# One fused attention and expert-mixture layer: the experts' maximum product widened to 64 rows, their softmax sums put on four groups of 32 columns

## The chip, the cores and the metric

The kernel runs on one core of a Trainium2 chip. The metric is device time in microseconds of one execution; for the kernel before, the median of three timed executions is 5184.0 us (5180.48 to 5186.56).

## The reference, cut to what matters

Thirty-two sequences of 512 tokens with 256 features go through a pre-norm attention layer with 16 heads of 16 and then a pre-norm layer of gated "expert" attention with 8 heads of 64:

```python
wv = topk_mask(gl_v, 2) * sigmoid(gl_v)                  # gates of the values, 5 experts a head
xv = einsum('btd,edk->btek', x, Wv)
v = einsum('bthe,btek->bhtk', wv, xv)
scores = einsum('bhid,bhjd->bhij', q * scale, k)          # 8 heads, 512 x 512
probs = softmax(scores, axis=-1)                          # maximum, exponential, sum
attn = einsum('bhij,bhjd->bihd', probs, v)
out = einsum('bthe,bthk,ekd->btd', mask_o, attn, Wo)
```

The two things that the change touches belong to this `softmax`: the row maxima, which are taken off before the exponential, and the row sums, by which the result is divided.

## The kernel before

One sequence is called a batch. A batch's work is cut into 16 slots, and the slots of neighbouring batches overlap like a pipeline: a list of slots, each of three thirds (g = 0, 1, 2), is walked through in the same order by all five engines, and each engine issues in every third what falls there. Semaphores tie the engines together; a small helper drops waits that were already satisfied. In this text, slot n of a batch is the one in which the experts' exponentials of its step n (of 16) are made; the steps are four pairs of heads times four blocks of 128 keys.

Per slot, TensorE makes in g = 0 and g = 1 one score tile of the first attention for exponentials (L209, into the double bank `expb`) and one for its maxima (L239, into `maxb`), then the products with the values (L263 for the first attention in g = 0, L274 for the experts in g = 1). In g = 2 it makes the experts' scores for the exponentials (L223, three products in split precision of 64 rows for each of two heads, which lie in rows 0 to 63 and 64 to 127), adds the negated maxima to the same accumulation (L227: a product of 2 rows, ones times the two parts of the maxima in `mrow`), and then makes the experts' scores for the maxima of a later step (L251). `expb` and `maxb` are each one buffer: ScalarE must have read `expb` (L429, L438) and VectorE `maxb` (the maxima, L560, L566) before the next product goes into it. Around these steps lie the projections, transposes and output products (L285 to L415), a few in each slot, which share two banks in turn.

Every fourth slot (n = 1, 5, 9, 13) has the sums of one pair of heads. GpSimd has added the exponentials over the keys (L741, into `acc`: 128 partitions, two heads, 512 queries). L382 sums over the partitions: for each of the 8 blocks of 128 queries it loads the block as weights and multiplies with a column of ones, so that the sums of 128 queries come out as one column, one query on each partition. VectorE takes the reciprocal of these 8 columns (L684, `rcf`) and multiplies it into the experts' weights (L689), and only then comes to the next maxima. The gate (top two of five, L636 to L671) is VectorE's work in slots n = 11 to 14; GpSimd then makes the gated values `vh` (L754, L759) that L274 reads from slot n = 1 on.

SyncE moves the maxima to HBM and back into `mrow` (L849, L854), and starts its loop after the constants are set (L803).

Of the kernel before, what the change touches and what calls it, by code (L numbers as in the profile page):

```python
# [36 lines left out]
def program(nc, t):  # L37
    F32, BF, F32R = mybir.dt.float32, mybir.dt.bfloat16, mybir.dt.float32r
# [3 lines left out]
    with ctx:  # L42
        def sb(name, shape, dt=F32):
            return ctx.enter_context(nc.sbuf_tensor("s_" + name, shape, dt))
# [32 lines left out]
        mrow = sb("mrow", [128, 2, 512], F32R)  # L77
# [11 lines left out]
        nmf = sb("nmf", [128, 4])  # L89
        prod = sb("prod", [128, 4, 2, 64])  # L90
        xf = sb("xf", [128, 2, 512])
        xg = sb("xg", [128, 4, 400])
        cg = sb("cg", [128, 10, 64])
        top = sb("top", [128, 6])
# [9 lines left out]
        ones = sb("ones", [128, 128], F32R)  # L104
        one = sb("one", [128, 1])
        mxf = sb("mxf", [128, 2, 4, 2])
# [88 lines left out]
        def tensor(e):  # L195
            w = Once(e)
            w.wait_ge(c_weights, 11 * 16)
            for s in SLOTS:
                for g in range(3):
# [12 lines left out]
                    if g == 2 and (r := part_of(s, F, 16)):  # L212
                        b, n = r
                        pair, kc = n // 4, n % 4
                        _, before = X.next(None, a_fexp, 16 * b + n + 1)
                        if before:
                            w.wait_ge(*before)
                        w.wait_ge(d_fr[pair], 32 * (b + 1))
                        t3, kk = (4 * b + pair) % 3, slice(128 * kc, 128 * kc + 128)
                        for kp, qp in ((hi, hi), (hi, lo), (lo, hi)):  # L220
                            for u in range(2):
                                ra = slice(64 * u, 64 * u + 64)
                                e.matmul(xb[:, u, :], kp[ra, t3, 1, kk], qp[ra, t3, 0, :],  # L223
                                         start=(kp is hi and qp is hi), stop=False)
                        for u in range(2):
                            ra = slice(64 * u, 64 * u + 2)
                            m = e.matmul(xb[:, u, :], ones[ra, :], mrow[ra, pair % 2, :], start=False, stop=True)  # L227
                        m.then_inc(p_fexp, 1)
# [25 lines left out]
                    if g == 0 and (r := part_of(s, 1, 16)):  # L254
# [4 lines left out]
                        if kc == 0:  # L259
                            w.wait_ge(c_vector, 4)  # L260
                            w.wait_ge(v_tr, 4 * b + j)
# [110 lines left out]
                    if r := pair_at(s, g, FS):  # L372
                        b, pair = r
                        n = 4 * b + pair
                        bk, before = R.next(("sum", b, pair), v_sum, n + 1)
                        if before:
                            w.wait_ge(*before)
                        w.wait_ge(c_pool, 3)
                        w.wait_ge(g_add, 6 * n + 6)
                        for u in range(2):  # L380
                            for i in range(4):
                                m = e.matmul(bk[:, 4 * u + i:4 * u + i + 1], acc[:, u, 128 * i:128 * i + 128], one[:, :],  # L382
                                             start=True, stop=True)
                        m.then_inc(p_acc, 1)
# [147 lines left out]
        def vector(e):  # L532
# [3 lines left out]
            e.memset(ks[96:128, :, :].bitcast(F32), 1.0).then_inc(c_vector, 1)  # L536
            e.memset(ones[:, :].bitcast(F32), 1.0).then_inc(c_vector, 1)

# [14 lines left out]
            for s in SLOTS:  # L553
                for g in range(3):
# [72 lines left out]
                    if r := at(s, g, [(27, 2), (28, 1), (29, 1), (29, 2), (30, 0)]):  # L627
                        b, k = r
                        gl = xg[:, :, 320:400].rearrange("p i (g e) -> p e i g", e=5)
                        cm = cg[:, :, :].rearrange("p c (i g) -> p c i g", i=4)  # L630
                        b0 = NG * b
                        w.wait_ge(a_xg, 4 * b + 4)
                        if k < 2:
                            for i in (2 * k, 2 * k + 1):
# [44 lines left out]
                    if r := pair_at(s, g, FS):  # L679
# [3 lines left out]
                        w.wait_ge(v_w, n)  # L683
                        e.reciprocal(rcf[:, :, :], R.at["sum", b, pair][:, 0:8].rearrange("p (u i) -> p u i", u=2)  # L684
                                     ).then_inc(v_sum, 1)
                        w.wait_ge(v_sum, n + 1)
                        if n > 1:
# [13 lines left out]
        def gpsimd(e):  # L701
# [9 lines left out]
            for s in SLOTS:  # L711
                for g in range(3):
# [29 lines left out]
                    if r := part_of(s, 30, 12):  # L742
# [4 lines left out]
                        if n == 0 or n % 2 == 1:  # L747
                            to = vv if n == 0 else prod[:, :, :, :]
                            w.wait_ge(v_gate, NG * b + NG)
# [7 lines left out]
                        else:  # L757
                            w.wait_ge(g_val, k)
                            e.tensor_tensor(vv, vv, prod[:, :, :, :], ALU.add).then_inc(g_val, 1)  # L759
                    for pair in range(4):  # L760
# [25 lines left out]
        def sync(e):  # L786
            w = Once(e)
            e.dma_start(xn[:, :, :], t["x"][0].rearrange("(c p) n -> p c n", p=128)).then_inc(d_xin, 16)
            for dst, src in [
# [12 lines left out]
                e.dma_start(dst, src).then_inc(c_weights, 16)  # L802
            w.wait_ge(c_vector, 4)  # L803
            for s in SLOTS:
                for g in range(3):
# [37 lines left out]
                    if r := pair_at(s, g, FT):  # L843
# [9 lines left out]
                        for u in range(2):  # L853
                            e.dma_start(mrow[64 * u:64 * u + 2, pair % 2, :].bitcast(F32), maxf[pair][:, u, :]  # L854
                                        ).then_inc(d_fr[pair], 16)
# [57 lines left out]
```

## Time and profile before

| what | value |
|---|---|
| median of 3 executions | 5184.0 us (5180.48 to 5186.56) |
| the profiled execution | 5176.93 us, of which the span of the trace is 5175.1 us |
| granted TensorE clock, mean over the span | 0.933 |
| PE busy | 4895.9 us, 95% |
| DVE busy | 3104.6 us, 60% |
| ACT busy | 2355.9 us, 46% |
| POOL busy | 3759.7 us, 73% |

PE is TensorE's matmuls, PEld its weight loads, DVE VectorE, ACT ScalarE, POOL GpSimd, SP SyncE. Matmuls are pipelined, so the busy time of PE counts their latencies too; the distance from one start to the next says more than the duration of one. A matmul of 32-bit floats stands in the trace as two records, one of the split-precision type as one.

### The profile page before, as it was taken

Reading aid. Unit: us, or ns where it says so; the run is one execution under the profiler, and the core shown is the slowest. Engines: PE = TensorE matmul, PEld = TensorE weight load, DVE = VectorE, ACT = ScalarE, POOL = GpSimd, SP = SyncE. Lnnn points to the kernel's source line nnn. Section 1 sums busy time; section 2 is a strip of 40 time slices with the busy share of each in tenths; the row PEclk is TensorE's granted clock in tenths of the full one; section 3 lists DMA queues with packets and bytes.
Section 4 is the critical chain, followed back from the end, with each engine's and each line's share of the span. In section 5 each row is a group of like instructions: output and inputs, shape, how many; then the busy total and the mean of one; then the engine's idle time right before and its main releaser. Section 6 shows DMA issues by size and latency. Waiting matters only on the chain.

```text
span 5175.1 us, 63686 instructions
## 1 busy us (share of the span) xinstructions
PE 4895.9 (95%) x23424; PEld 2131.0 (41%) x23424; DVE 3104.6 (60%) x4164; ACT 2355.9 (46%) x3073; POOL 3759.7 (73%) x3149
## 2 busy tenths in 40 slices
PE   5889999999999999999999999999999999999986
PEld 2234444444444444444444444444444444444343
DVE  4566666666666666666666666656666656666431
ACT  2444444444444444444444445444444444444421
POOL 0057777877777777777787777787777787777898
PEclk7799999999999999999999999999999999999987
DMA  3211111111111111111111112111111111111000
GB/s 90 66 51 41 44 51 41 51 45 54 44 42 45 46 45 55 44 41 54 37 48 52 44 41 55 36 51 49 45 44 51 37 54 45 52 44 32 10 5 9
DMA packets 158502, 231.58 MB, mean 45 GB/s; under 512 B 21680, under 2 KB 72688, under 8 KB 158192
## 3 DMA queue, kind: packets, MB, share of 16 engines
q1 hardware_dynamic: 158192, 227.51, 15.4%
q8 instruction: 186, 3.05, 0.2%
q14 instruction: 124, 1.02, 0.1%
HBM read 140.39 MB, written 87.03 MB: 44 GB/s over the span
## 4 chain that ended last, share of the span: by engine, by line
PE 80%; DVE 12%; POOL 3%; ACT 2%; issue 2%; DMA 1%; SPq 0%; POOLq 0%; ACTq 0%; DVEq 0%
PE bank L369 9%; PE ofb L274 9%; PE oab L263 9%; PE expb L223 8%; PE expb L209 6%; PE maxb L239 6%; PE bank L296 5%; PE bank L382 5%; PE maxb L251 4%; PE bank L415 4%; DVE s_mxa L560 4%; PE expb L227 4%; PE bank L349 4%; DVE s_mxf L566 4%; PE bank L329 3%; PE bank L317 2%
## 5 line engine op out<-in xcount | busy, mean ns | idle before, releaser
L560 DVE TENSOR_REDUCE s_mxa<-maxb 128x2 f32<-128x1024 f32 x1024 | 1247.8, 1219 | 348.1 <-PE maxb L239 347.1
L429 ACT ACTIVATE s_pa<-expb 128x1024 f32<-128x1024 f32 x1024 | 1052.8, 1028 | 411.7 <-PE expb L209 399.2
L438 ACT ACTIVATE s_pf<-expb 128x1024 f32<-128x1024 f32 x512 | 524.9, 1025 | 1033.1 <-PE expb L227 1026.4
L566 DVE TENSOR_REDUCE s_mxf<-maxb 128x2 f32<-128x1024 f32 x512 | 627.0, 1225 | 593.5 <-PE maxb L251 592.4
L741 POOL TENSOR_TENSOR s_acc<-s_acc,s_pf 128x512 f32<-128x512 f32 x512 | 661.5, 1313 | 117.6 <-ACT s_pf L438 117.6
L741 POOL TENSOR_TENSOR s_acc<-s_pf 128x512 f32<-128x512 f32 x256 | 320.5, 1274 | 527.7 <-ACT s_pf L438 527.7
L774 POOL TENSOR_TENSOR s_uu<-s_uu,s_pu 128x640 f32<-128x640 f32 x448 | 693.4, 1548 | 11.0
L759 POOL TENSOR_TENSOR s_vh<-s_vh,s_prod 128x512 f32<-128x512 f32 x512 | 652.8, 1275 | 15.5
L263 PE MATMUL oab<-s_pa,s_v 128*17 128x512 f32 x4096 | 614.7, 676 | 0.0
L239 PE MATMUL maxb<-s_ks,s_qs 48*128 48x512 f32 x2048 | 483.3, 457 | 138.0 <-DVE s_mxa L560 97.0
L274 PE MATMUL ofb<-s_pf,s_vh 128*64 128x512 f32 x2048 | 564.0, 629 | 32.0 <-POOL s_vh L759 22.0
L209 PE MATMUL expb<-s_qs,s_ks 50*128 50x512 f32 x2048 | 557.0, 530 | 28.4 <-ACT s_pa L429 10.1
L780 POOL TENSOR_TENSOR s_pu<-s_ots,s_w 128x640 f32<-128x640 f32 x448 | 574.6, 1283 | 2.9
L754 POOL TENSOR_TENSOR s_prod<-s_xg,s_wvx 128x512 f32<-128x512 f32 x512 | 543.3, 1061 | 13.1
L209 PEld LDWEIGHTS expb<-s_qs,s_ks 50*128 50x128 f32 x2048 | 207.1, 194 | 575.7 <-issue 399.8
L579 DVE TENSOR_TENSOR s_lo<-bank,s_hi 128x512 fp32r<-128x512 f32 x256 | 177.1, 692 | 374.6 <-ACT s_hi L446 374.6
L715 POOL TENSOR_TENSOR s_rsa<-s_vea,s_nhalf 128x4 f32<-128x4 f32 x32 | 32.6, 1018 | 393.4 <-DVE s_nma L550 380.1
L446 ACT CAST s_hi<-bank 128x512 fp32r<-128x512 f32 x256 | 150.2, 587 | 365.0 <-PE bank L369 365.0
L239 PEld LDWEIGHTS maxb<-s_ks,s_qs 48*128 48x128 f32 x2048 | 212.6, 199 | 247.4 <-DVE s_mxa L560 150.6
L382 PEld LDWEIGHTS bank<-s_one,s_acc 128*128 128x128 f32 x2048 | 247.0, 197 | 121.2 <-DVE s_lo L579 96.6
L251 PE MATMUL maxb<-s_hi 64*128 64x512 f32 x1024 | 267.7, 520 | 23.0 <-DVE s_mxa L560 22.0
L223 PE MATMUL expb<-s_hi 64*128 64x512 f32 x1024 | 276.8, 514 | 0.7 <-DMA s_mrow<-w_maxf 0.2
(106 smaller groups left out, 6655.3 us busy)
## 6 DMA issues: line engine op xcount, KB each, us to landing
w_parts<-s_pt SPq DMA_DIRECT2D x128, 512.0 KB, 2.9
s_qs<-w_parts SPq DMA_DIRECT2D x256, 128.0 KB, 3.2
s_ks<-w_parts SPq DMA_DIRECT2D x256, 128.0 KB, 3.1
s_xn<-in_x SPq DMA_DIRECT2D x32, 512.0 KB, 4.7
s_qs<-w_parts SPq DMA_DIRECT2D x256, 64.0 KB, 3.2
s_ks<-w_parts SPq DMA_DIRECT2D x256, 64.0 KB, 3.0
s_xa<-in_x SPq DMA_DIRECT2D x32, 512.0 KB, 4.6
out_y<-s_xa SPq DMA_DIRECT2D x32, 512.0 KB, 2.9
```

The costliest lines, as they stand in the source:

```text
L209: m = e.matmul(xb[:, a, :], ks[64 * a:64 * a + 50, pr, 128 * kc:128 * kc + 128], qs[64 * a:64 * a + 50, pr, :], start=True, stop=True)
L223: e.matmul(xb[:, u, :], kp[ra, t3, 1, kk], qp[ra, t3, 0, :], start=(kp is hi and qp is hi), stop=False)
L239: m = e.matmul(mb[:, a, :], qs[64 * a:64 * a + 48, pr, 128 * i:128 * i + 128], ks[64 * a:64 * a + 48, pr, :], start=True, stop=True)
L263: m = e.matmul(oa[32 * h:32 * h + 17, :], v32[:, b % 2, kc, 4 * j + h, :], pa[:, (32 * b + 2 * n + h // 2) % 3, h % 2, :], start=(kc == 0) ...
L274: m = e.matmul(of[64 * u:64 * u + 64, :], vh[:, kc, 2 * pair + u, :], pf[:, (16 * b + n) % 3, u, :], start=(kc == 0), stop=(kc == 3))
L429: e.activation(pa[:, k % 3, :, :], xb[:, :, :], ACT.Exp, scale=0.0625).then_inc(a_aexp, 1)
L560: e.tensor_reduce(mxa[:, c, k % 4, 2 * (k // 4):2 * (k // 4) + 2], mb[:, :, :], AX.X, ALU.max, negate=True).then_inc(v_amax, 1)
L566: e.tensor_reduce(mxf[:, pair % 2, i, :], mb[:, :, :], AX.X, ALU.max, negate=True).then_inc(v_fmax, 1)
L741: e.tensor_tensor(acc[:, u, :], was, pf[:, k % 3, u, :], ALU.add).then_inc(g_add, 1)
L759: e.tensor_tensor(vv, vv, prod[:, :, :, :], ALU.add).then_inc(g_val, 1)
L774: e.tensor_tensor(uu[:, cut, :], uu[:, cut, :], pv, ALU.add).then_inc(g_mix, 1)
L780: e.tensor_tensor(to.rearrange("p i (e k) -> p i e k", k=64), ots[:, n % 2, cut, 64 * u:64 * u + 64].unsqueeze(2).to_broadcast([128, 2, 5, ...
```

## The change

L227 becomes a product of 64 rows: a new tile `mx` of 128 rows holds zeros but for rows 0, 1, 64 and 65, to which SyncE now brings the maxima, and `ones` is zero but for the same four rows. L382 swaps its operands: the stationary one is a tile of ones with 32 columns, and the moving one is `acc`, of which each quarter of every block of 128 queries goes to its own group of 32 columns; the sums of a head then stand as rows, 32 copies of each, in the four quarters of the partitions. VectorE turns them with a transpose of 32 by 32 blocks into `t1` and takes the reciprocal from there. Room for `mx` is made by letting the gate's tile `cg` share memory with GpSimd's `prod`, with a wait in the gate for it; the constants need three more memsets.

```diff
-        prod = sb("prod", [128, 4, 2, 64])
+        prod = sb("prod", [128, 640])
+        cg = prod[:, :].rearrange("p (c g) -> p c g", g=64)
+        prod = prod[:, 0:512].rearrange("p (i u k) -> p i u k", i=4, u=2)
-        cg = sb("cg", [128, 10, 64])
-        one = sb("one", [128, 1])
+        one = sb("one", [128, 32])
+        mx = sb("mx", [128, 2, 512], F32R)
...
-                            ra = slice(64 * u, 64 * u + 2)
-                            m = e.matmul(xb[:, u, :], ones[ra, :], mrow[ra, pair % 2, :], start=False, stop=True)
+                            ra = slice(64 * u, 64 * u + 64)
+                            m = e.matmul(xb[:, u, :], ones[ra, :], mx[ra, pair % 2, :], start=False, stop=True)
...
-                        bk, before = R.next(("sum", b, pair), v_sum, n + 1)
+                        bk, before = R.next(("sum", b, pair), v_sum, 2 * n + 1)
...
                         for u in range(2):
-                            for i in range(4):
-                                m = e.matmul(bk[:, 4 * u + i:4 * u + i + 1], acc[:, u, 128 * i:128 * i + 128], one[:, :],
-                                             start=True, stop=True)
+                            rows = acc[:, u, :].rearrange("p (i q t) -> p q i t", i=4, q=4)
+                            for q in range(4):
+                                m = e.matmul(bk[32 * q:32 * q + 32, 128 * u:128 * u + 128].rearrange(
+                                    "p (i t) -> p i t", i=4), one[:, :], rows[:, q, :, :], start=True, stop=True)
...
-            e.memset(ones[:, :].bitcast(F32), 1.0).then_inc(c_vector, 1)
+            e.memset(ones[:, :].bitcast(F32), 0.0).then_inc(c_vector, 1)
+            e.memset(mx[:, :, :].bitcast(F32), 0.0).then_inc(c_vector, 1)
+            w.wait_ge(c_vector, 4)
+            e.memset(ones[0:2, :].bitcast(F32), 1.0).then_inc(c_vector, 1)
+            e.memset(ones[64:66, :].bitcast(F32), 1.0).then_inc(c_vector, 1)
...
+                        w.wait_ge(g_val, 36 * b)
...
-                        e.reciprocal(rcf[:, :, :], R.at["sum", b, pair][:, 0:8].rearrange("p (u i) -> p u i", u=2)
+                        e.transpose(t1[:, 0, 0:256], R.at["sum", b, pair][:, 0:256]).then_inc(v_sum, 1)
+                        w.wait_ge(v_sum, 2 * n + 1)
+                        e.reciprocal(rcf[:, :, :], t1[:, 0, 0:256].rearrange("p (u i t) -> p u i t", u=2, t=32)[:, :, :, 0]
                                      ).then_inc(v_sum, 1)
-                        w.wait_ge(v_sum, n + 1)
+                        w.wait_ge(v_sum, 2 * n + 2)
...
-                            e.dma_start(mrow[64 * u:64 * u + 2, pair % 2, :].bitcast(F32), maxf[pair][:, u, :]
+                            e.dma_start(mx[64 * u:64 * u + 2, pair % 2, :].bitcast(F32), maxf[pair][:, u, :]
                                         ).then_inc(d_fr[pair], 16)
```

The waits of TensorE and SyncE for VectorE's constants go from 4 to 7.

## Rows read from the trace of the kernel before

**Rows 1.** The page, part 4: the chain that ended last, by engine.
```profile
PE 80%; DVE 12%; POOL 3%; ACT 2%; issue 2%; DMA 1%; SPq 0%; POOLq 0%; ACTq 0%; DVEq 0%
```

**Rows 2.** Busy time by stretch: PE, PEld, DVE, ACT, POOL, then clock, DMA, GB/s.
```profile
500.00:2500.00 2000.00, 1949.74 (x9502) 851.05 (x9501) 1253.76 (x1689) 953.69 (x1245) 1523.76 (x1273) 0.96 0.16 46
...
4950.00:5000.00 50.00, 47.69 (x199) 23.76 (x198) 19.65 (x20) 16.35 (x25) 49.29 (x40) 0.91 0.03 12
```

**Rows 3.** One batch's matmuls of L227: count, durations, first and last start.
```profile
L227 PE MATMUL expb<-s_mrow,s_ones x34: 489/497/613, 2456.1 to 2609.7; 2*128 2x512 f32 x34
```

**Rows 4.** Timeline of PE, third g = 2 of slot 5: start, length, instruction.
```profile
2508.49 0.51 PE L223 MATMUL expb<-s_hi 64*128 64x512 f32 x2
2508.83 0.40 PE L223 MATMUL expb<-s_lo,s_hi 64*128 64x512 f32 x2
2509.06 0.39 PE L223 MATMUL expb<-s_hi,s_lo 64*128 64x512 f32 x2
2509.38 0.50 PE L227 MATMUL expb<-s_mrow,s_ones 2*128 2x512 f32 x2
2509.81 0.50 PE L251 MATMUL maxb<-s_hi 64*128 64x512 f32 x2
2510.25 0.66 PE L392 MATMUL bank<-s_ident,s_osb 128*128 128x128 f32 x4
```

**Rows 5.** Timeline of PE, thirds g = 0 and 1 of slot 5.
```profile
2501.71 0.40 PE L239 MATMUL maxb<-s_ks,s_qs 48*128 48x512 f32 x2
2502.04 1.05 PE L263 MATMUL oab<-s_pa,s_v 128*17 128x512 f32 x8
2503.02 0.70 PE L369 MATMUL bank<-s_xf,s_fk 128*128 128x512 f32 x1
...
2506.62 1.95 PE L382 MATMUL bank<-s_one,s_acc 128*128 128x1 f32 x16
```

**Rows 6.** Groups by line, whole span: busy us, mean ns, idle before and releaser.
```profile
L263 PEld LDWEIGHTS oab<-s_pa,s_v 128*17 128x17 f32 x4096 | 69.8, 98 | 180.0 <-issue 180.0
...
L597 DVE STREAM_TRANSPOSE s_t<-oab 128x512 f32<-128x512 f32 x128 | 90.2, 704 | 3.5 <-PE oab L263 3.5
```

**Rows 7.** Timeline of DVE and of PE, slot 13 (sums and gate).
```profile
2583.93 0.22 DVE L649 TENSOR_TENSOR s_rk<-s_rk,s_cg 128x64 f32<-128x64 f32 x1
...
2584.30 0.22 DVE L689 TENSOR_TENSOR s_w<-s_mask,s_rcf 128x40 f32<-128x40 f32 x1
2585.50 1.23 DVE L566 TENSOR_REDUCE s_mxf<-maxb 128x2 f32<-128x1024 f32 x1 [0.98 <-PE maxb L251]
...
2583.64 0.50 PE L223 MATMUL expb<-s_hi 64*128 64x512 f32 x2
```

**Rows 8.** Busy time and clock by stretch, after sums; and one sum block.
```profile
2354.53:2361.36 6.83, 6.83 (x27) 1.86 (x24) 3.75 (x4) 4.25 (x7) 6.06 (x5) 0.50 0.03 5
...
2467.17:2474.00 6.83, 6.83 (x24) 3.23 (x23) 2.45 (x2) 2.64 (x3) 6.83 (x7) 0.50 0.00 0
...
2503.00:2517.00 14.00, 13.76 (x82) 6.51 (x78) 8.03 (x10) 7.57 (x11) 11.58 (x10) 1.00 0.19 33
...
2464.16 1.95 PE L382 MATMUL bank<-s_one,s_acc 128*128 128x1 f32 x16
```

**Rows 9.** Timeline: L227 of slots 5 and 6 of one batch, slot 6 of the next.
```profile
2353.24 0.50 PE L227 MATMUL expb<-s_mrow,s_ones 2*128 2x512 f32 x2
...
2363.16 0.50 PE L227 MATMUL expb<-s_mrow,s_ones 2*128 2x512 f32 x2
...
2516.69 0.50 PE L227 MATMUL expb<-s_mrow,s_ones 2*128 2x512 f32 x2
```

**Rows 10.** Timeline: GpSimd's last values of a pair, and the product that reads them.
```profile
2614.56 1.26 POOL L759 TENSOR_TENSOR s_vh<-s_vh,s_prod 128x512 f32<-128x512 f32 x1
...
2616.67 1.08 PE L274 MATMUL ofb<-s_pf,s_vh 128*64 128x512 f32 x4
```

**Rows 11.** Waits of weight loads, 500 to 4500 us: total us, times, longest.
```profile
PEld maxb L251 <- DVE s_mxa L560: 25.6, 52, 0.7
```

More of the change, by code:

```diff
@@ L259, in tensor @@
                         if kc == 0:
-                            w.wait_ge(c_vector, 4)
+                            w.wait_ge(c_vector, 7)
                             w.wait_ge(v_tr, 4 * b + j)
@@ L629, in vector @@
                         gl = xg[:, :, 320:400].rearrange("p i (g e) -> p e i g", e=5)
-                        cm = cg[:, :, :].rearrange("p c (i g) -> p c i g", i=4)
+                        cm = cg.rearrange("p c (i g) -> p c i g", i=4)
                         b0 = NG * b
                         w.wait_ge(a_xg, 4 * b + 4)
+                        w.wait_ge(g_val, 36 * b)
                         if k < 2:
@@ L747, in gpsimd @@
                         if n == 0 or n % 2 == 1:
-                            to = vv if n == 0 else prod[:, :, :, :]
+                            to = vv if n == 0 else prod
                             w.wait_ge(v_gate, NG * b + NG)
@@ L758, in gpsimd @@
                             w.wait_ge(g_val, k)
-                            e.tensor_tensor(vv, vv, prod[:, :, :, :], ALU.add).then_inc(g_val, 1)
+                            e.tensor_tensor(vv, vv, prod, ALU.add).then_inc(g_val, 1)
                     for pair in range(4):
@@ L802, in sync @@
                 e.dma_start(dst, src).then_inc(c_weights, 16)
-            w.wait_ge(c_vector, 4)
+            w.wait_ge(c_vector, 7)
             for s in SLOTS:
```

## The prediction

> **What bounds the kernel now.** I read the chain that ended last first: TensorE holds four fifths of it, VectorE an eighth [rows 1]. The busy times by stretch say that this holds over the whole steady part (TensorE 1950 of 2000 us) and that GpSimd, at 1524, is next [rows 2]. Only the last two batches are different: there GpSimd is busy 49.3 of 50 us [rows 2], and TensorE's savings will not count. So I look at distances between starts on TensorE in the other 30 batches, each 153.6 us long [rows 3], and then ask, slot by slot, what would hold TensorE up if it came earlier: VectorE's maxima, GpSimd's values. Last, the clock: its mean is 0.96 in the steady stretch [rows 2], so about 8% of the time, some 12.3 us of each batch, runs at 1.2 instead of 2.4 GHz, and it matters where.
>
> **The maximum rows (L227).** Two products of 64 rows run side by side on the two halves of the array, and the next pair follows 0.23 us later (2508.83 to 2509.06). To L227, a product of 2 rows, the distance is 0.32 us, from it to L251, again of 64 rows, 0.43 [rows 4]. The three products of L223, with different operands but all of 64 rows, have no such break between them; it stands on both sides of the one whose rows are others, so I take it that 64 rows close it. Then L227 starts at 2509.29, L251 at 2509.52, 0.29 us earlier than it did; and L251, no longer freshly started, is followed by its successor after 0.33 instead of 0.44 (L239 to L263: 2501.71 to 2502.04 [rows 5]), another 0.11. Bounds: nothing if the cause is another one, 0.40 if nothing waits. The 0.29 reaches the end wherever L251 is not waiting for VectorE; it waits in 52 of some 417 slots (4000 / 153.6 x 16), 0.49 us each [rows 11], which is two a batch. I count one of the two as lost, the other as a short wait, so 15 of 16 slots: 4.35 us a batch. The later 0.11 is lost where TensorE then waits for the maxima of L251 or for ScalarE's exponential, which is so in the slots with a short block behind L251; I count half of the slots: 0.9. Together 5.2 us a batch.
>
> **The sums (L382).** Now a block takes from 2506.62 to 2508.49, 1.87 us [rows 4, 5]: 16 records, each with a load of 128 columns and one moving column. The nearest row for the new form is L263: it too is of 32-bit floats, on four groups of columns side by side, two records each of 512 columns, and takes 0.98 us to the next line's start [rows 5]. Of this I put 0.20 to the change of shape (0.43 against 0.23 in [rows 4]), which leaves 0.78 for 2 x 512 columns. The new block has 4 records of 128 columns in each group, 512 in all: 0.39 + 0.20 = 0.59 us. Bounds: 0.49, if all of L263 shrinks with its columns, and 1.87, if the groups do not overlap. I take 0.59, by L263; it saves 1.28 us a block, 5.1 us a batch.
>
> Eight loads of 98 ns each [rows 6] and 0.78 us of streaming do not fit into L263's 0.98 us one after the other: loads and products overlap there. The Trainium skill ("TensorE: Matmul & The Clock Gate", Part 3, the mechanism) says that a weight load overlaps with running products only if it goes to another group of rows. All groups of the new block use all rows, and by that rule four loads of 98 ns would stand in the open: 0.98 us a block instead of 0.59. This trace does not agree; it is a rival below.
>
> **What VectorE adds.** One transpose of 256 columns: the one of 512 takes 704 ns [rows 6], so between 0.35 and 0.70; I take 0.45, as part of the 0.70 is not per column. With one more wait, it lies between the sums and L689, and L566 is queued behind it; TensorE's next score tile waits for L566. In slots 1, 5 and 9, where VectorE has little else, L251 follows the block by 1.03 us and its maxima can be taken 0.54 later (2583.64 + 1.32 to 2585.50 in [rows 7]), and this hides it; without that cover it would cost 0.45 a block. In slot 13 it doesn't: L566 began at 2585.50, waiting for L251. With everything above, L223 would start at 2582.36 instead of 2583.64, L251 1.03 later, and its maxima could be taken at 2583.93. But the gate's operations end at 2584.15 whatever TensorE does [rows 7]; then come transpose (0.45), the reciprocal and its waits (0.25) and L689 (0.22): L566 at about 2585.05. This slot gains 0.45 instead of 1.57: 1.1 us a batch lost again.
>
> **GpSimd.** It works without a pause from the gate's end until `vh` is ready at 2615.82, and L274 reads it at 2616.67 [rows 10]: 0.85 us of room. TensorE's path over the three slots between gets shorter by 0.11 + 0.40 + 0.40 = 0.91, so I take off 0.1 us a batch. The shared memory of `cg` and `prod` costs nothing: ScalarE's copies for the gate already wait for the same values, and the gate waits for the copies. The memsets delay the start by some 2 us, once, as the loads of the weights cover most of it. The maxima's transfer is of the same size and only lands elsewhere. SyncE's queue is passed by nothing.
>
> At the same clock, this is 5.2 + 5.1 - 1.1 - 0.1 = 9.1 us a batch, times 30: 273 us.
>
> **The clock.** The two falls shown begin right after a sum block: at 2467.17, where the block ran from 2464.16 to about 2466.0, and at 2354.53, after slot 5's [rows 8]. In such a block the array gets 16 columns in 1.87 us. With the fall, slots 5 to 6 are 9.92 us apart (2353.24 to 2363.16); without it, one batch later, 7.31 (2509.38 to 2516.69) [rows 4, 8, 9]: 2.61 us for 6.83 us at the lower level, 0.38 each. With the new form the array gets 512 columns on all groups within 0.6 us, and the products around it come closer, so I expect the falls after sums to go. Bounds: nothing, and 12.3 x 0.38 = 4.7 us a batch. I take three quarters, 3.5, since behind the gate VectorE sets the pace whatever the clock is: 105 us.
>
> **The sum.** 273 + 105 = 378, less 2 at the start. It is worked out on the profiled execution: a span of 5175.1 in 5176.93 us, 7 below the median of the timed ones; I take it off the median: 5184 - 376 = 4808, say **4810 us**.
>
> **Rivals.** (a) *The clock's falls stay*, because the waits for VectorE do to it what the sums did. For it: they become longer, not shorter. Against it: 2503 to 2517 contains short waits and a sum block at full clock [rows 8]. 4810 + 105 = 4915. (b) *L227's break is not due to its rows*, that is, this part does nothing. For it: L227 also differs from L223 in where its operand comes from, by a transfer. Against it: a transfer could delay its start, not that of L251 behind it, and the longer break is there [rows 4]. 5.2 x 30 = 156 more, 4966. (c) *Loads in the open*: 0.39 x 3 blocks x 30 = 35 more, 4845. This is the Trainium skill's rule above. (d) *VectorE stands in the way in all four sum slots* as in slot 13, from other work that I have not lined up: 1.1 x 3 x 30 = 99 more, 4909. (e) *Slower*: the array is fed in bursts that are shorter and waits that are longer, the clock falls in the middle of light slots, and the falls feed on themselves, as a slow TensorE also starts VectorE later. With 273 us gained, and the 30 x 4.7 = 141 us that the falls cost now, it decides from (273 + 141) / 0.38 = 1090 us at the lower level within the 4600 us of the 30 batches, a mean clock under 0.88; at 0.80 (1840 us) it would be 5184 + 1840 x 0.38 - 414 = 5469. For it: the last stretch of [rows 2], where TensorE waits for GpSimd, has 0.91. Against it: the array loses idle time, not work.
>
> **How the numbers follow.** My forecast 0.56, with its own range 4760 to 4870 (sum block 0.49 or 0.75 us, falls priced fully or by half); (a) 0.13, (b) 0.06, (c) 0.09, (d) 0.10, (e) 0.03, two of (a) to (d) together 0.03. All but (e) are faster. A difference under 0.2% could not be told from none here. The range for eight in ten goes at the low end to the case in which nothing is absorbed (1.2 x 30 = 36 for slot 13 and GpSimd, 36 for the falls): 4738; at the high end to (b): 4970. Faster 0.95, same 0.02, slower 0.03.
>
> **What the profile after would show.** L227 0.23 us after L223's last pair, and L251 0.23 after it; otherwise (b). The sum block 0.5 to 0.6 us long; at 0.98 it is (c), at 1.8 the groups do not overlap, and the forecast is wrong by 150 us. Mean clock over the steady stretch 0.99 or 1.00, with no fall behind a sum; otherwise (a). L566 in slot 13 right behind L689, with no wait for TensorE. Transposes of about 450 ns. GpSimd's busy time unchanged, its idle time smaller by the saving; if `vh` L759 becomes what L274 waits for by more than 0.3 us, GpSimd has become a bound and the saving is smaller.

## The result and the profile after

The kernel after takes 4798.44 us (median of 4 executions, 4797.92 to 4804.66), the one before on the same chip 5182.24 us (5177.27 to 5186.56): a ratio of 0.9262 [0.9246, 0.9278], 7.4% faster. The forecast was 4810. The profiled execution took 4798.16 us, its span is 4796.4.

The page of the kernel after, in part: the span, part 1 (busy time) and part 4 (the chain that ended last, by engine).

```profile
span 4796.4 us, 63817 instructions
...
PE 4400.0 (92%) x23424; PEld 1886.8 (39%) x23424; DVE 3179.6 (66%) x4295; ACT 2335.3 (49%) x3073; POOL 3761.9 (78%) x3149
...
PE 66%; DVE 18%; POOL 6%; ACT 5%; issue 4%; DMA 0%; SPq 0%; POOLq 0%; ACTq 0%; DVEq 0%
```

TensorE is busy for 496 us less than in the table of before, VectorE for 75 more, GpSimd for as long as it was. TensorE's share of the chain goes from 80% to 66%, VectorE's from 12% to 18% [rows 1]: VectorE is in the way more often now, and it matters where.

The busy time by stretch, columns as in [rows 2], and one batch's products of the maxima (L230, before L227), from slot 1 to the next batch's slot 1, as in [rows 3]:

```profile
500.00:2500.00 2000.00, 1906.95 (x10348) 820.40 (x10348) 1399.51 (x1889) 1028.14 (x1355) 1663.67 (x1387) 0.99 0.18 50
```

```profile
L230 PE MATMUL expb<-s_mx,s_ones x34: 383/387/392, 2430.2 to 2571.2; 64*128 64x512 f32 x34
```

The batch takes 141.0 us where it took 153.6 [rows 3], and the clock's mean is 0.99 where it was 0.96 [rows 2]. The timeline of PE in slot 1, from the sum block (L387, before L382) on; each line is start, length, instruction, as in [rows 4]:

```profile
2428.84 0.64 PE L387 MATMUL bank<-s_acc,s_one 128*32 128x128 f32 x16
2429.42 0.50 PE L226 MATMUL expb<-s_hi 64*128 64x512 f32 x2
2429.75 0.39 PE L226 MATMUL expb<-s_lo,s_hi 64*128 64x512 f32 x2
2429.98 0.40 PE L226 MATMUL expb<-s_hi,s_lo 64*128 64x512 f32 x2
2430.22 0.40 PE L230 MATMUL expb<-s_mx,s_ones 64*128 64x512 f32 x2
2430.45 0.40 PE L254 MATMUL maxb<-s_hi 64*128 64x512 f32 x2
2430.78 0.66 PE L397 MATMUL bank<-s_ident,s_osb 128*128 128x128 f32 x4
```

Read the distances of the starts. The sum block takes 0.58 us (2428.84 to 2429.42), before 1.87. From the last L226 to L230 it is 0.24, on to L254 0.23, and on to L397 0.33; in [rows 4] the same three were 0.32, 0.43 and 0.44. So both edits do on TensorE what the forecast says, to 0.01 us.

What differs from the forecast stands on VectorE in slot 13, where sums and gate meet. First the timeline of DVE, then of POOL, then of PE, and last the busy time of the stretch that follows.

```profile
2395.28 0.23 DVE L659 TENSOR_TENSOR s_rk<-s_rk,s_prod 128x64 f32<-128x64 f32 x1
2395.42 0.44 DVE L694 STREAM_TRANSPOSE s_t<-bank 128x256 f32<-128x256 f32 x1
2395.90 0.20 DVE L696 RECIPROCAL s_rcf<-s_t 128x8 f32<-128x8 f32 x1
2396.14 1.20 DVE L701 TENSOR_TENSOR s_w<-s_mask,s_rcf 128x40 f32<-128x40 f32 x1
2397.26 1.21 DVE L575 TENSOR_REDUCE s_mxf<-maxb 128x2 f32<-128x1024 f32 x1
```

```profile
2396.01 2.49 POOL L753 TENSOR_TENSOR s_acc<-s_pf 128x512 f32<-128x512 f32 x2 [9.24 <-ACT s_pf L443]
```

```profile
2393.68 0.50 PE L226 MATMUL expb<-s_hi 64*128 64x512 f32 x2
...
2398.53 0.51 PE L242 MATMUL maxb<-s_ks,s_qs 48*128 48x512 f32 x2 [2.03 <-DVE s_mxf L575]
```

```profile
2399.13:2402.54 3.41, 3.41 (x16) 0.85 (x8) 1.83 (x4) 0.64 (x2) 0.00 (x0) 0.50 0.00 0
```

L701, 40 elements wide, took 0.22 us here before (L689 in [rows 7]) and takes 1.20 now. GpSimd's two adds (L753) began 0.13 us ahead of it, and it ends at 2397.34, about when the first of the two does (2396.01 + 2.49 / 2 = 2397.26). The maxima (L575) stand behind it, TensorE's next score tile (L242) waits 2.03 us for them, and 0.6 us after the wait's end the clock goes to 0.50, that is from 2.4 to 1.2 GHz, for 3.41 us. Such a stretch is called a fall below. I counted falls and steps from slot to slot (from one L230 to the next) in the trace of each kernel, over 28 batches. In the kernel after, all falls stand behind slot 13, in 23 of 28 batches between its L230 and the next; that step then takes 10.53 us (median) instead of 9.15. The wait before it is the same, 2.03 to 2.05 us, in the five batches without a fall, and why these five differ is not shown. Before, the lower level held for 13.9 us a batch, mostly behind slots 0, 1, 5 and 13; now for 3.4.

### The profile page after: what moved, and what is told of

The parts are those of the page before. It is cut to its first block, busy times and chain, and to the rows that moved or that the text cites. A ratio compares the mean times of both kernels' runs of the same rounds, so it can differ in the third digit from the quotient of the medians.

```text
span 4796.4 us, 63817 instructions
## 1 busy us (share of the span) xinstructions
PE 4400.0 (92%) x23424; PEld 1886.8 (39%) x23424; DVE 3179.6 (66%) x4295; ACT 2335.3 (49%) x3073; POOL 3761.9 (78%) x3149
## 4 chain that ended last, share of the span: by engine, by line
PE 66%; DVE 18%; POOL 6%; ACT 5%; issue 4%; DMA 0%; SPq 0%; POOLq 0%; ACTq 0%; DVEq 0%
PE bank L372 9%; PE oab L266 9%; DVE s_mxa L569 7%; PE ofb L277 7%; PE expb L226 6%; PE maxb L242 5%; PE expb L212 5%; PE bank L299 5%; PE bank L352 4%; PE bank L420 4%; DVE s_mxf L575 3%; PE bank L320 3%; ACT s_pf L443 3%; PE bank L332 2%; PE maxb L254 2%
## 5 line engine op out<-in xcount | busy, mean ns | idle before, releaser
L575 DVE TENSOR_REDUCE s_mxf<-maxb 128x2 f32<-128x1024 f32 x512 | 625.4, 1221 | 268.0 <-PE maxb L254 256.9
L753 POOL TENSOR_TENSOR s_acc<-s_acc,s_pf 128x512 f32<-128x512 f32 x512 | 675.5, 1340 | 11.2 <-ACT s_pf L443 9.8
L242 PE MATMUL maxb<-s_ks,s_qs 48*128 48x512 f32 x2048 | 476.2, 450 | 162.1 <-DVE s_mxf L575 72.9
L212 PE MATMUL expb<-s_qs,s_ks 50*128 50x512 f32 x2048 | 536.9, 510 | 79.9 <-ACT s_pf L443 68.1
L753 POOL TENSOR_TENSOR s_acc<-s_pf 128x512 f32<-128x512 f32 x256 | 320.6, 1274 | 326.7 <-ACT s_pf L443 326.7
L266 PE MATMUL oab<-s_pa,s_v 128*17 128x512 f32 x4096 | 563.3, 623 | 0.0
L242 PEld LDWEIGHTS maxb<-s_ks,s_qs 48*128 48x128 f32 x2048 | 206.8, 194 | 278.1 <-DVE s_mxf L575 140.2
L766 POOL TENSOR_TENSOR s_vh<-s_xg,s_wvx 128x512 f32<-128x512 f32 x128 | 135.5, 1058 | 219.0 <-DVE s_wvx L681 219.0
L226 PE MATMUL expb<-s_hi 64*128 64x512 f32 x1024 | 271.5, 504 | 1.8 <-ACT s_pa L434 1.5
L372 PE MATMUL bank<-s_xf,s_fq 128*128 128x512 f32 x512 | 253.9, 618 | 0.0
```

What stands on the lines that cost most here:

```text
L212: m = e.matmul(xb[:, a, :], ks[64 * a:64 * a + 50, pr, 128 * kc:128 * kc + 128], qs[64 * a:64 * a + 50, pr, :], start=True, stop=True)
L242: m = e.matmul(mb[:, a, :], qs[64 * a:64 * a + 48, pr, 128 * i:128 * i + 128], ks[64 * a:64 * a + 48, pr, :], start=True, stop=True)
L266: m = e.matmul(oa[32 * h:32 * h + 17, :], v32[:, b % 2, kc, 4 * j + h, :], pa[:, (32 * b + 2 * n + h // 2) % 3, h % 2, :], start=(kc == 0) ...
L372: m = e.matmul(bk[:, :], (fq, fk)[z][:, f, 128 * pair:128 * pair + 128], xf[:, f, :], start=(f == 0), stop=(f == 1))
L575: e.tensor_reduce(mxf[:, pair % 2, i, :], mb[:, :, :], AX.X, ALU.max, negate=True).then_inc(v_fmax, 1)
L753: e.tensor_tensor(acc[:, u, :], was, pf[:, k % 3, u, :], ALU.add).then_inc(g_add, 1)
```

## The experiments

All times are medians; each ratio is to the kernel before on the same chip.

**One part alone.** The first kernel is the one before with the 64 rows (and `mx`, the memsets and the shared `cg`), the second is the one before with the new sums and the transpose.

```diff
-                            ra = slice(64 * u, 64 * u + 2)
-                            m = e.matmul(xb[:, u, :], ones[ra, :], mrow[ra, pair % 2, :], start=False, stop=True)
+                            ra = slice(64 * u, 64 * u + 64)
+                            m = e.matmul(xb[:, u, :], ones[ra, :], mx[ra, pair % 2, :], start=False, stop=True)
...
```

> The kernel before with the first part alone: the maxima as a product of 64 rows, the sums as they were. Theory (the break is the change of the rows' group, and the clock falls after sum blocks): L227's part is worth 5.2 us a batch, so about 156 us less than before, some 5026 us; the sum block stays at 1.87 us and the mean clock in the steady part at 0.96. Rival (the break has another cause): no change, 5182 us, and 0.32 and 0.43 us around the product as before. Rival (the clock falls at the breaks, not at the sums): clock near 0.99 and 5026 less some 100 us.

```diff
+                            rows = acc[:, u, :].rearrange("p (i q t) -> p q i t", i=4, q=4)
+                            for q in range(4):
+                                m = e.matmul(bk[32 * q:32 * q + 32, 128 * u:128 * u + 128].rearrange(
+                                    "p (i t) -> p i t", i=4), one[:, :], rows[:, q, :, :], start=True, stop=True)
...
+                        e.transpose(t1[:, 0, 0:256], R.at["sum", b, pair][:, 0:256]).then_inc(v_sum, 1)
```

> The kernel before with the second part alone: the sums on four groups of columns and VectorE's transpose, the maxima as a product of 2 rows. Theory: block of 0.57 us instead of 1.87, 5.1 us a batch less, 1.1 of it lost in slot 13 to VectorE, and the falls of the clock after sums gone (3.5 us a batch): (5.1 - 1.1 + 3.5) x 30 = 225 us less, some 4957 us, clock 0.99. Rival (the falls are not tied to the sums): clock 0.96 and 105 us more, 5062 us. If the two parts add up, the savings of this run and of the one with the first part alone make the 384 us measured for both.

The rows alone: 4960.37 us, 0.9558 [0.9538, 0.9577], 222 less than before. The sums alone: 4940.31, 0.9526 [0.951, 0.9542], 243 less. Together that is 465, and the whole change brings 384. The busy time by stretch of the first and then of the second tells why:

```profile
500.00:2500.00 2000.00, 1924.60 (x9984) 884.91 (x9982) 1330.22 (x1774) 997.28 (x1313) 1594.51 (x1328) 0.98 0.17 48
```

```profile
500.00:2500.00 2000.00, 1920.99 (x10000) 788.18 (x10000) 1354.43 (x1833) 1005.15 (x1314) 1597.28 (x1332) 0.99 0.17 49
```

Both lift the clock, from 0.96 to 0.98 and 0.99, where I had expected the rows to leave it alone; why they lift it, no run shows. In the batches counted, the lower level holds for 6.3 us a batch with the rows alone, 2.4 with the sums alone and 3.4 with both, of 13.9 before.

What the falls cost can be told from the steps. The sum of the 16 steps of a batch, of each the median of those that hold no fall, is its time at full clock; the rest of the mean batch is the cost of the falls. (Before, a fall stands in every step behind slot 1 of these batches; its 8.68 us are from the batch behind them.)

| kernel | mean batch, us | at full clock, us | cost of the falls, us |
|---|---|---|---|
| before | 154.04 | 150.07 | 3.97 |
| rows alone | 146.80 | 145.16 | 1.64 |
| sums alone | 146.37 | 145.67 | 0.70 |
| both | 141.64 | 140.45 | 1.19 |

At full clock the parts nearly add: 4.91 and 4.40 us, and 9.62 for both. The falls are what they share: of 3.97 us the rows save 2.33, the sums 3.27 and both 2.78, so 2.82 x 30 = 85 us are counted twice, near the 81 that are missing. The falls before cost 3.97 us for 13.9 at the lower level, 0.29 each, where the forecast has 0.38 from one place.

**Columns behind the loads.** The kernel before, but each of the 16 records of a sum block moves 64 columns of ones behind its 128-column load, where it was one; the rest of the block is the same, and VectorE reads each 64th column.

```diff
-        one = sb("one", [128, 1])
+        one = sb("one", [128, 64])
...
-                                m = e.matmul(bk[:, 4 * u + i:4 * u + i + 1], acc[:, u, 128 * i:128 * i + 128], one[:, :],
+                                m = e.matmul(bk[:, 64 * (4 * u + i):64 * (4 * u + i) + 64], acc[:, u, 128 * i:128 * i + 128], one[:, :],
```

> The kernel before, but each block of sums is multiplied with 64 columns of ones instead of one (VectorE reads each 64th column). The loads of 128 columns, which set the block's 1.87 us, stay, and 64 columns stream beside them. Theory (the clock falls because the array gets only 16 columns in a sum block): the block keeps 1.9 us, the falls after sums go, the clock rises from 0.96 to about 0.99, and the time falls by up to 105 us, to some 5080 us. Rival (the falls come from something else, or the block's breaks): clock 0.96 and 5182 us; or the block gets longer by the columns, 16 x 0.05 us, and the time grows by 100 us.

5092.2 us, 0.9807 [0.9777, 0.9838]. Its group of L382 and its busy time by stretch:

```profile
L382 PE MATMUL bank<-s_one,s_acc 128*128 128x64 f32 x2048 | 265.0, 284 | 12.1 <-POOL s_acc L741 12.1
```

```profile
500.00:2500.00 2000.00, 1925.18 (x9624) 842.39 (x9626) 1282.55 (x1703) 965.25 (x1262) 1545.31 (x1290) 0.99 0.17 47
```

The products are no shorter (284 ns, with one column 256), more columns are moved, and the kernel is 91 us faster: the lower level goes from 13.9 to 2.8 us a batch. So the falls behind a sum block came with what it did, not with the work after it. The estimate of 0.38 per us gives (13.9 - 2.8) x 0.38 x 30 = 127 us, more than the 91. The longer block is 6 us of the difference (1.93 us instead of 1.88, four times in 30 batches); the rest is the price. Counted by steps as above, the mean batch goes from 154.04 to 151.84, at full clock from 150.07 to 150.27, and the falls cost 1.57 instead of 3.97: 2.40 us for 11.1 at the lower level, 0.22 each.

**Rows of the array.** The kernel after with L230 on 32 rows, and on 33. The rows beyond the two of the maxima hold zeros.

```diff
-                            ra = slice(64 * u, 64 * u + 64)
+                            ra = slice(64 * u, 64 * u + 32)
```

> The changed kernel with 32 rows instead of 64 in the product of the maxima (rows 0 to 31 and 64 to 95; the left-out rows are zeros). Theory (another group of rows breaks the stream): the breaks of 0.32 and 0.43 us come back, and 5.2 us a batch, 156 us: some 4955 us. Rival (the breaks had to do with the tile that the maxima came from, or with products of only 2 rows): 4798 us, as changed.

```diff
-                            ra = slice(64 * u, 64 * u + 64)
+                            ra = slice(64 * u, 64 * u + 33)
```

> The changed kernel with 33 rows instead of 64 in the product of the maxima, one more than in the run with 32. Theory (what counts is the group of rows that the product is put into, and more than 32 rows share that of 64): no break, 0.23 us on both sides, 4798 us. Rival (any number of rows other than that of the neighbours breaks the stream): 4955 us, like 32 rows.

32 rows: 4931.71, 0.9512 [0.9491, 0.9532]. 33 rows: 4802.39, 0.927 [0.9256, 0.9284], as with 64. The timeline of PE with 32, then with 33:

```profile
2496.61 0.40 PE L226 MATMUL expb<-s_hi,s_lo 64*128 64x512 f32 x2
2496.94 0.50 PE L230 MATMUL expb<-s_mx,s_ones 32*128 32x512 f32 x2
2497.37 0.50 PE L254 MATMUL maxb<-s_hi 64*128 64x512 f32 x2
2497.80 0.66 PE L397 MATMUL bank<-s_ident,s_osb 128*128 128x128 f32 x4
```

```profile
2430.05 0.39 PE L226 MATMUL expb<-s_hi,s_lo 64*128 64x512 f32 x2
2430.28 0.39 PE L230 MATMUL expb<-s_mx,s_ones 33*128 33x512 f32 x2
2430.51 0.40 PE L254 MATMUL maxb<-s_hi 64*128 64x512 f32 x2
```

With 32 rows the two breaks are back (0.33 and 0.43 us, in [rows 4] 0.32 and 0.43), with 33 they are gone (0.23, 0.23). One row decides, so it is the group of rows that a product takes, not its operands or how many rows it shares with its neighbours. The Trainium skill ("TensorEngine Tiling (Array Packing)", Key Properties) says that a change of the tiling mode, not merely of the tile, drains TensorE; the trace agrees, and puts 0.40 us of distance on a product that goes to another mode and back (0.10 before it, 0.20 behind it, and 0.10 on to the next, which follows L254 after 0.43 with 32 rows and after 0.33 in the kernel after).

**A second transpose.** The kernel after, with the transpose done again into an unused half of `t1`.

```diff
+                        e.transpose(t1[:, 0, 256:512], R.at["sum", b, pair][:, 0:256])
```

> The changed kernel with VectorE's transpose of the sums done twice (the extra one into the unused half of its tile). Theory (hidden in slots 1, 5 and 9, in the open in slot 13, where VectorE's queue is full): 0.45 us x 30 = 13 us more, about 4812 us. Rival (in the way in all four slots): 0.45 x 4 x 30 = 54 us more, 4852 us. Rival (hidden everywhere): 4798 us.

4833.84 us, 0.9331 [0.9313, 0.9349]: 35 more than the kernel after, between the two. By slots it is neither theory. Slot 9 loses nothing (7.91 us to the next L230 in both). Slot 1 loses 0.69 (8.53 to 9.22), slot 5 0.32. Slot 13 is no longer than it was where the clock holds (9.15, in one batch), but a fall stands behind it in 27 of 28 batches, and then it takes 11.67; why in more of them, no run shows. Slot 1 in this kernel, DVE and PE; the last line is the same place in the kernel after.

```profile
2447.26 0.41 DVE L694 STREAM_TRANSPOSE s_t<-bank 128x256 f32<-128x256 f32 x1
2447.59 0.41 DVE L695 STREAM_TRANSPOSE s_t<-bank 128x256 f32<-128x256 f32 x1
...
2448.27 0.65 DVE L702 TENSOR_TENSOR s_w<-s_mask,s_rcf 128x40 f32<-128x40 f32 x1
2448.84 1.21 DVE L575 TENSOR_REDUCE s_mxf<-maxb 128x2 f32<-128x1024 f32 x1
```

```profile
2450.11 0.50 PE L242 MATMUL maxb<-s_ks,s_qs 48*128 48x512 f32 x2 [0.86 <-DVE s_mxf L575]
```

```profile
2432.40 0.50 PE L242 MATMUL maxb<-s_ks,s_qs 48*128 48x512 f32 x2 [0.17 <-DVE s_mxf L575]
```

The second transpose adds 0.33 us to VectorE and 0.69 to TensorE's wait: the weights' product (here L702) is longer too, 0.65 us. And the 0.17 of the kernel after says that its own transpose is not fully hidden in this slot.

**The weights' product on GpSimd.** The kernel after, with L701 issued by GpSimd, in g = 0 of the next slot behind its adds, and `rcf` doubled.

```diff
-                        e.tensor_tensor(w2[:, n % 2, :, :, :],
...
+                    if r := pair_at(s, g, (F + 6, 0)):
...
+                        e.tensor_tensor(w2[:, n % 2, :, :, :],
```

> The changed kernel with the experts' weights (reciprocals times mask, 40 elements, the operation that took 1.21 us in slot 13 while GpSimd added exponentials) made by GpSimd, one slot later, instead of VectorE; the reciprocals get a second buffer. Rival theory (VectorE's queue before the maxima is what slot 13 waits for): the maxima come 1.1 us earlier and 1.1 x 30 = 33 us are saved, 4765 us. Theory (behind it the gate's operations wait for GpSimd's adds anyway): under 10 us saved, 4790 to 4798 us; GpSimd's own 128 x 0.25 us cost nothing.

4748.04 us, 0.9166 [0.9152, 0.918], 50 less than the kernel after and the fastest version of all. My theory, less than 10, fell, and the rival's 33 were too few. Slot 13 again, on DVE, POOL and PE:

```profile
2506.12 0.20 DVE L696 RECIPROCAL s_rcf<-s_t 128x8 f32<-128x8 f32 x1
2506.24 1.18 DVE L575 TENSOR_REDUCE s_mxf<-maxb 128x2 f32<-128x1024 f32 x1
...
2507.51 1.31 DVE L662 TENSOR_TENSOR s_rk<-s_rk,s_prod 128x64 f32<-128x64 f32 x1
```

```profile
2506.23 2.50 POOL L746 TENSOR_TENSOR s_acc<-s_pf 128x512 f32<-128x512 f32 x2 [8.91 <-ACT s_pf L443]
2508.69 0.27 POOL L753 TENSOR_TENSOR s_w<-s_mask,s_rcf 128x40 f32<-128x40 f32 x1
```

```profile
2507.47 0.50 PE L242 MATMUL maxb<-s_ks,s_qs 48*128 48x512 f32 x2 [0.77 <-DVE s_mxf L575]
...
2511.03 0.49 PE L242 MATMUL maxb<-s_ks,s_qs 48*128 48x512 f32 x2 [1.11 <-DVE s_mxa L569]
```

GpSimd's adds still hold VectorE up, but now it is the gate's L662 (1.31 us, otherwise 0.21), behind the maxima. TensorE's one wait of 2.03 us has become two, of 0.77 and 1.11. The slot is hardly shorter (9.10 us, against 9.15 where the clock holds in the kernel after), but it falls in none of 28 batches, where that one did in 23 and took 10.53. That is 23 / 28 x 1.38 + 0.05 = 1.2 us a batch; slots 1 and 5 give 0.25 and 0.28, for L701 stood in their way too (8.53 to 8.28, 7.17 to 6.89). 1.7 x 30 = 51 us.

**Less work for GpSimd.** The kernel after, with GpSimd's adds cut to 32 of 512 columns.

```diff
-                            e.tensor_tensor(acc[:, u, :], was, pf[:, k % 3, u, :], ALU.add).then_inc(g_add, 1)
+                            e.tensor_tensor(acc[:, u, 0:32], was, pf[:, k % 3, u, 0:32], ALU.add).then_inc(g_add, 1)
```

> The changed kernel with GpSimd's additions of exponentials cut to the first 32 of 512 columns (the rest of the sums are not made; the tile is set once). GpSimd's work falls by some 24 x 1.2 us a batch of 117. Theory (GpSimd's adds hold up VectorE's operations on two tiles of SBUF in slot 13, and its chain to the values is within 0.6 us of holding up TensorE): 1.5 to 3 us a batch, 45 to 90 us less, 4710 to 4755 us, and the experts' weights take 0.22 us everywhere. Rival (GpSimd holds up nothing): 4798 us, but for the last two batches, where GpSimd is busy throughout (2 x 24 x 1.2 = 58 us at most).

4820.02 us, 0.9314 [0.9292, 0.9336]: slower than the kernel after, though GpSimd is busy for 23% less (1280.32 us of the stretch from 500 to 2500, with the full adds 1663.67). Neither theory has that. Slots 5 and 13 did get shorter (7.17 to 6.90, 10.52 to 8.66 us in the mean), but slot 1 went from 8.53 to 13.59. Its DVE, POOL and PE:

```profile
2471.05 4.22 DVE L701 TENSOR_TENSOR s_w<-s_mask,s_rcf 128x40 f32<-128x40 f32 x1
2475.19 1.21 DVE L575 TENSOR_REDUCE s_mxf<-maxb 128x2 f32<-128x1024 f32 x1
```

```profile
2471.02 1.27 POOL L772 TENSOR_TENSOR s_vh<-s_vh,s_prod 128x512 f32<-128x512 f32 x1
2472.25 1.53 POOL L787 TENSOR_TENSOR s_uu<-s_uu,s_pu 128x640 f32<-128x640 f32 x1
2473.73 0.46 POOL L754 TENSOR_TENSOR s_acc<-s_pf 128x32 f32<-128x32 f32 x2
2474.15 1.06 POOL L767 TENSOR_TENSOR s_prod<-s_xg,s_wvx 128x512 f32<-128x512 f32 x1
2475.29 1.26 POOL L772 TENSOR_TENSOR s_vh<-s_vh,s_prod 128x512 f32<-128x512 f32 x1
```

```profile
2476.46 0.79 PE L242 MATMUL maxb<-s_ks,s_qs 48*128 48x512 f32 x2 [4.10 <-DVE s_mxf L575]
```

L701 started 0.03 us after GpSimd's L772 and got through only when GpSimd had its first gap, between 2475.21 and 2475.29: 4.22 us for 40 elements, five instructions of GpSimd long. TensorE waited 4.10 us for the maxima behind it. The Trainium skill ("SBUF — State Buffer", Who interferes with whom) says that VectorE's operations with two inputs in SBUF contend with GpSimd's instructions that read SBUF, for a port under an exclusive lock, and that reductions do not. The rows agree: L575, a reduction, took at most 1.23 us in all 512 cases. But here L701 was held up across five instructions, not one, and so it was in 20 of 28 batches (4.21 to 4.25 us; in seven it took 1.3). What decides how many is not shown. A gap of GpSimd is not always needed: in slot 13 of the kernel after, L701 got through 0.06 us behind the end of the first of two adds that followed one another without one.

**Three more, on another chip.** The weights' product moved to GpSimd in the kernel before; and, on top of the fastest version, the second transpose, and the sums' transpose and reciprocal put behind the maxima.

> The kernel before with only the experts' weights moved to GpSimd, as in the run that moved them in the changed kernel (50 us there). Theory (the stall behind GpSimd came with the change, as the sums are ready when GpSimd is busy; before, the operation took 0.22 us in three of four slots and 0.57 in the fourth): no more than the operation's own time, 0.22 to 0.57 us hidden behind L251, so 5170 to 5182 us, and the clock 0.96 as before. Rival (the move is worth 50 us in any kernel): 5132 us.

> The changed kernel with the weights on GpSimd, and the transpose done twice. In the changed kernel the second transpose cost 36 us, in slots 1, 5 and 13. Theory (the cover that hides a transpose was eaten by the stalled operation behind it): hidden in slots 1 and 5 now, in the open in slot 13 at most, 0 to 13 us more than 4748, 4748 to 4761 us. Rival (transposes are in the open in themselves): 36 us more, 4784 us.

> The changed kernel with the weights on GpSimd, and VectorE's transpose and reciprocal behind the maxima of the same slot instead of in front of them. Theory (VectorE's queue in slot 13 is full up to the next maxima but one, whose gate operations wait for GpSimd): the maxima of slot 13 come 0.6 us earlier and the ones after them do not; 0 to 10 us less than 4748. Rival (each 0.6 us in front of the maxima counts): 0.6 us in slot 13 and some in slots 1 and 5, 20 to 40 us less, 4710 to 4730 us.

In the kernel before, the move brings 0.16%, 5166.42 us at 0.9984 [0.9975, 0.9992]: the 50 us were not there to be had, the stall came with the change. The lower level held there for 10.5 us a batch instead of 13.9, and the mean batch is only 0.49 us shorter (153.55): what 1 us at the lower level costs is no constant. In [rows 7], L689 was through at 2584.52, and this is where GpSimd's adds began in that kernel, and what they held up (POOL, DVE, then PE):

```profile
2586.18 2.52 POOL L741 TENSOR_TENSOR s_acc<-s_pf 128x512 f32<-128x512 f32 x2 [11.41 <-ACT s_pf L438]
```

```profile
2586.65 0.89 DVE L651 TENSOR_TENSOR s_rk<-s_rk,s_cg 128x64 f32<-128x64 f32 x1
2587.46 1.31 DVE L652 TENSOR_TENSOR s_rk<-s_rk,s_cg 128x64 f32<-128x64 f32 x1
```

```profile
2590.89 0.51 PE L239 MATMUL maxb<-s_ks,s_qs 48*128 48x512 f32 x2 [1.66 <-DVE s_mxa L560]
```

The adds were in the way of the gate, behind the maxima. Count from the gate's operation that runs just ahead of the sums: L689 began 0.37 us after L649 did (2583.93 to 2584.30, [rows 7]), the adds 2.25. In the kernel after, L701 begins 0.86 us after L659 (2395.28 to 2396.14), as the transpose lies between, and the adds 0.73, since TensorE's products and so the exponentials come earlier. So the two met.

The second transpose on the fastest version: 4772.6, 0.9225 [0.9213, 0.9237], where that version had 0.9166. It is between the theories; the steady batches are 0.4 us longer (140.29 to 139.89, which is 12 us), mostly slot 1 (8.28 to 8.50) and falls behind slot 13 in 3 batches of 28. The profiled executions differ by 24 us, of which another 5 lie ahead of the 28 batches and 7 behind them; why, I have not found. Sums behind the maxima: 4753.28, 0.9193 [0.9177, 0.9209], 0.3% above the fastest version, so no gain: slots 1, 5 and 9 stayed as they were (8.29, 6.90, 7.91).

## Why the prediction was right, and where it was not

The forecast of 4810 was 12 us off. It said 9.1 us a batch at the same clock and 3.5 by the clock, 12.6; from L230 to L230 the mean batch went from 154.04 to 141.64, 12.4 less, of which 9.6 at full clock and 2.8 by the falls.

- **The 64 rows, 5.2 us a batch: right.** The breaks closed as forecast. At full clock the rows alone save 4.9. 32 rows instead of 64 make the batch 4.36 us longer (146.00 to 141.64), with 1.95 us less at the lower level; at 0.29 each that is 4.36 + 0.57 = 4.9, too. Rival (b) is out by the runs with 32 and 33 rows. What I missed is that this part alone also lifts the clock. That 64 rows close the break was read off products of 64 rows; that 33 are enough I did not foresee.
- **The sum block, 0.59 us: right,** 0.58. Loads in the open, rival (c), would have been 0.98. All 16 weight loads of the block stand in the first 0.38 us of its 0.58, beside the products that began with the first of them, though all groups use all rows (the line of PEld for the block of slot 1):

```profile
2428.84 0.38 PEld L387 LDWEIGHTS bank<-s_acc,s_one 128*32 128x32 f32 x16 [0.81 <-DVE s_lo L588]
```

- **VectorE's transpose.** 434 ns in the mean for 450. That it is hidden in slots 1, 5 and 9 holds in the kernel after in slot 9 alone. Where the clock holds, the slots take 8.53, 7.17, 7.91 and 9.15 us (n = 1, 5, 9, 13) and with the rows alone 8.29, 6.90, 7.92 and 9.03: 0.24 + 0.27 + 0 + 0.12 = 0.6 us a batch is what the new sums cost through VectorE. I had 1.1, all of it in slot 13. With L701 on GpSimd slots 1 and 5 are back at 8.28 and 6.89, so there it was the transpose and L701 together that did not fit.
- **Slot 13: the step that failed.** "L689 (0.22): L566 at about 2585.05" was L701 at 1.20. From L226's start to that of the maxima I had 2.69 us (2585.05 - 2582.36), and it is 3.58 (2397.26 - 2393.68): 0.89 more, and L701 alone took 0.98 more than I gave it. I took its duration from a row that had GpSimd's adds behind it, and did not ask where they would stand once everything came earlier. It cost little directly, as VectorE had been held up in this slot before (L651 and L652). It cost by the clock: one wait of 2.03 us and a fall behind it, in place of shorter waits. Moving that one instruction to GpSimd gave 50 us.
- **The clock, 3.5 us a batch: too much, and for reasons that I had half.** The lower level fell by three quarters, as I had it (13.9 to 3.4 us, where I had started from 12.3), but its price of 0.38 came from one pair of slots; the falls cost 2.8 less (3.97 to 1.19). No fall is left behind slots 0, 1, 5 and 9, and what is left stands behind the gate, where I said it would. Rival (a) holds there alone.
- **GpSimd, 0.1 us: right.** It is busy for 3761.9 us, before 3759.7, and `vh` held no product up in the 28 batches. Rival (d), VectorE in all four slots, is true in a small way: in slots 1 and 5 at a quarter of a microsecond each, which is half a microsecond a batch where it asked for 3.3. Rival (e) did not come: the clock rose.

So the forecast had 0.5 too little at full clock (9.1 for 9.6, mostly because the sums cost less through VectorE) and 0.7 too much by the clock (3.5 for 2.8). That the two nearly cancel, and the total is 12 us off, is luck; that the rows and the sum block bring what they do is not. The clock's term stays the softest: before, a fall behind slot 13 cost nothing (9.21 us with one, 9.23 without), and elsewhere 1 us at the lower level cost 0.14 to 0.38.

## What to carry to other kernels

Look at which rows of the array neighbouring products use: one that falls into another group of rows costs its neighbours' overlap, and zeros up to the group's size are cheaper than that. When a stage gets shorter, line up again what the other engines do beside it: a VectorE operation of two SBUF operands that was 0.22 us in the old place may stand behind GpSimd in the new one, and if the next tile's maxima wait behind it, it is worth moving. Ask of every wait that is left on TensorE whether the clock falls behind it, since two short waits here cost less than one long one.

## What was not expected of the hardware

- A product of 33 rows runs in step with its neighbours of 64, one of 32 does not: 4802.39 against 4931.71 us.
- A sum block with 64 times the columns and products of 284 instead of 256 ns makes the kernel 91 us faster, because the clock falls less behind it.
- A VectorE operation of 40 elements took 4.22 us beside five instructions of GpSimd in a row, in a kernel whose GpSimd is busy for 23% less and which is 22 us slower.
- Behind a wait of 2.03 us of TensorE, with VectorE as its cause, the clock fell in 23 of 28 batches, and with the same wait not in five; with two waits of 0.77 and 1.11 us in its place, in none.
